# Two-head score steps on two row groups, half-plane maxima, shared mix banks and one pool of eight banks in a four-layer transformer kernel

## The reference, cut to what matters

```python
# block 0 and 1: self attention, cross attention, MLP   (layers 0,1,7 and 2,3,8 of the kernel)
# block 2: cross attention                              (layer 4)
# block 3: windowed self attention, top-k cross attention, SwiGLU   (layers 5, 6, 9)
attn = softmax(einsum('bhnd,bhsd->bhns', q, k) * scale)       # 256 x 256 per head
o = einsum('bhns,bhsd->bhnd', attn, v)
# layer 5: four windows of 64 rows, shifted by 32
# layer 6: top_s, top_i = lax.top_k(scores, 16); softmax over those 16; weighted sum of their v
```

## Time and profile before

| what | value |
|---|---|
| time, three runs | 828.72, 837.08, 854.2 us (median 837.08) |
| span of the profiled execution | 830.0 us, mean granted TensorE clock 0.751 |
| PE / DVE / ACT / POOL busy | 694.1 / 519.2 / 405.8 / 240.4 us |

### The profile page before, as it was taken

The page is one execution under the profiler, slowest core; times in us unless marked ns, Lnnn a source line. Parts: engine busy times, 40 slices in busy tenths (PEclk is TensorE's granted clock), DMA queues, the critical chain, the costliest instruction groups (busy, mean ns, idle before and its releaser), DMA issues.

```text
span 830.0 us, 14443 instructions
## 1 busy us (share of the span) xinstructions
PE 694.1 (84%) x5066; PEld 470.7 (57%) x5066; DVE 519.2 (63%) x1455; ACT 405.8 (49%) x677; POOL 240.4 (29%) x471
## 2 busy tenths in 40 slices
PE   4899997899899898989899887997688968866755
PEld 3675554566566565666566655665555645544533
DVE  3366466635456564646551567778876889899931
ACT  3234555476827476755656570574044713533321
POOL 7511113232333124242112330235010721521302
PEclk9557577798969698969786985597556975886866
DMA  9620203111312401040402060006000220020000
GB/s 346 191 51 3 52 6 65 35 32 23 69 37 52 103 2 43 15 101 8 97 2 53 2 153 1 3 2 145 8 3 1 53 57 3 1 59 0 2 7 6
DMA packets 21700, 39.22 MB, mean 47 GB/s; under 512 B 2496, under 2 KB 6656, under 8 KB 21248
## 3 DMA queue, kind: packets, MB, share of 16 engines
q1 hardware_dynamic: 20912, 37.82, 18.5%
q10 hardware_dynamic: 720, 0.49, 0.2%
HBM read 7.96 MB, written 0.52 MB: 10 GB/s over the span
## 4 chain that ended last, share of the span: by engine, by line
PE 56%; DVE 21%; POOL 7%; DMA 5%; issue 5%; ACT 4%; SPq 2%; POOLq 0%; ACTq 0%; DVEq 0%
PE score L979 14%; PE misc L1025 13%; PE wide L1002 8%; DVE maxima L860 4%; PE wide L1061 4%; DVE left L874 3%; DVE left L882 3%; DVE top L879 3%; PE wide L1036 3%; DVE top L871 3%; DMA qk_stack<-centred 2%; DMA qk_stack<-qk_parts 2%; PE misc L1072 2%; ACT softmax_T L757 2%; SPq L584 2%
## 5 line engine op out<-in xcount | busy, mean ns | idle before, releaser
L860 DVE TENSOR_REDUCE maxima<-score 128x2 f32<-128x512 f32 x320 | 211.8, 687 | 149.0 <-PE score L979 148.0
L757 ACT ACTIVATE softmax_T<-wide 128x1024 f32<-128x1024 f32 (+1 forms) x224 | 211.2, 968 | 106.3 <-PE wide L1002 54.1
L979 PE MATMUL score<-qk_stack 32*128 32x256 f32 (+1 forms) x896 | 215.4, 387 | 53.1 <-DVE maxima L860 20.9
L979 PEld LDWEIGHTS score<-qk_stack 32*128 32x128 f32 x896 | 145.4, 241 | 125.2 <-DVE maxima L860 45.4
L1025 PE MATMUL misc<-softmax_T,values 128*32 128x256 f32 (+1 forms) x1792 | 145.4, 450 | 9.8 <-issue 5.8
L1002 PE MATMUL wide<-qk_stack 32*128 32x256 f32 (+1 forms) x896 | 130.6, 389 | 17.4 <-DMA qk_stack<-centred 9.1
L1002 PEld LDWEIGHTS wide<-qk_stack 32*128 32x128 f32 x896 | 88.3, 240 | 63.4 <-issue 36.3
L686 POOL TENSOR_SCALAR unpicked<-left 128x512 bf16<-128x512 f32 x64 | 39.5, 617 | 191.0 <-DVE left L882 155.1
L1025 PEld LDWEIGHTS misc<-softmax_T,values 128*32 128x32 f32 x1792 | 62.0, 128 | 50.4 <-issue 28.7
L768 ACT ACTIVATE mixed_T<-misc 128x256 f32<-128x256 f32 x112 | 43.6, 389 | 62.0 <-PE misc L1025 61.6
L764 ACT ACTIVATE centred<-misc 16x256 f32<-16x256 f32 (+1 forms) x40 | 14.8, 370 | 104.0 <-PE misc L990 77.8
(11 more groups left out here) (95 smaller groups left out, 802.7 us busy)
## 6 DMA issues: line engine op xcount, KB each, us to landing
qk_stack<-qk_parts SPq DMA_DIRECT2D x112, 256.0 KB, 4.7
weights<-in_w SPq DMA_DIRECT2D x1, 2368.0 KB, 18.3
weights<-in_w SPq DMA_DIRECT2D x1, 1408.0 KB, 13.1
row_biases<-in_rows SPq DMA_DIRECT2D x1, 1088.0 KB, 10.3
weights<-in_w SPq DMA_DIRECT2D x1, 832.0 KB, 8.7
x<-in_x SPq DMA_DIRECT2D x1, 512.0 KB, 4.7
context<-in_ctx SPq DMA_DIRECT2D x1, 512.0 KB, 7.1
out<-x SPq DMA_DIRECT2D x4, 128.0 KB, 2.1
```

The source lines that it names most:

```text
L757: nc.scalar.activation(pT[:, slot, u % 2, :, 0:cols], wide[:, SLOT["wide", step], :, 0:cols], ACT.Exp).then_inc(fin, 1)
L860: nc.vector.tensor_reduce(rows[:, u // 4, u % 4, :], ps.rearrange("p (t k) -> p t k", t=NT), AX_X, ALU.max).then_inc(fin, 1)
L979: ins = nc.tensor.matmul(ps[:, at:at + (P if window else N)], QKS[b][32 * g:32 * g + 32, s, 0, P * t:P * t + P], QKS[b][32 * g:32 * g + 32 ...
```

## The change

- **Score steps of two heads.** `scores` and `topk` steps now take two heads on two neighbouring row groups, 1024 columns in two banks; the four matmuls are written tile by tile with the row groups alternating. 16 steps of a full layer become 8, 8 of the window layer 4, 16 of the top-k layer 8. DVE reduces 1024 columns in one instruction; in top-k each of the four kinds of instruction comes four times in a row. The window layer's `weights` steps go from 8 to 4, of two planes each. The `weights` matmuls alternate row groups too.
- **Maxima in halves.** In full and window layers the maxima of planes 0, 1 and of planes 2, 3 go back separately: two times two transposes, a copy of 8 rows and a DMA, each half with its own semaphore. They are staged in `mixed_T` rather than in `centred`.
- **Two planes share a mix bank.** `values` holds each head in 18 columns (nine and nine zeros), so that two planes add into one bank with 18 used rows per row group. ACT copies twice per layer rather than four times, `divide` takes four transposes rather than eight, and its DVE product is two instructions rather than one.
- **One pool of eight banks.** `wide`, `score` and `misc` become `banks`; a step takes any free bank or pair. The plan lets one scores or topk step be unread at a time (`SCORES_HOLD`) and two mix banks (`MIX_HOLD`). `softmax_T` has three slots, the mask ring two steps of two heads, `context_centred` two slots.
- **The plan.** New costs, a PE cost that depends on a modelled clock, and tables `FIRST` and `EARLY` that shift priorities by kind, batch and layer. The statistics of the context are taken once rather than for each of layers 1 and 4.

```diff
-SLOTS = {"misc": 2, "wide": 2, "score": 2, "qk": 2, "pt": 2, "left": 2, "nm": 8}
+SLOTS = {"qk": 2, "pt": 3, "left": 2, "nm": 2, "zc": 2}
+BANKS.update({k: 2 for k in ("scores", "topk", "weights", "up", "up_gate")})
+SCORES_HOLD, MIX_HOLD = 1, 2
...
+EARLY = [[-23, 13, -73, 16, 45, -31, -10, 13, 0, 113],
...
-LEAD = (120.0, 80.0, 40.0, 0.0)
+LEAD = (141.0, 94.0, 31.0, 23.0)
...
                 elif kind == "scores":
...
-                        nc.vector.tensor_reduce(rows[:, u // 4, u % 4, :], ps.rearrange("p (t k) -> p t k", t=NT), AX_X,
+                        nc.vector.tensor_reduce(mx[:, b, :, first:first + 3:2].rearrange("p t g -> p g t"),
+                                                pair_of(step).rearrange("p g (t k) -> p g t k", t=NT), AX_X,
                                                 ALU.max).then_inc(fin, 1)
...
                 elif kind in ("scores", "topk"):
-                    ps = score[:, SLOT["score", step], :]
-                    g = u % 4
+                    ps = pair_of(step)
+                    planes, groups = heads_of(l, u)
...
                         for t in range(NT):
+                            for g in groups:
...
+                                    to, keys = ps[:, g % 2, N * t:N * t + N], slice(0, N)
+                                ins = nc.tensor.matmul(to, QKS[b][32 * g:32 * g + 32, s, 0, P * t:P * t + P],
+                                                       QKS[b][32 * g:32 * g + 32, s, 1, keys], start=True, stop=True)
...
-                            ins = nc.tensor.transpose(misc[0:NH, P * t:P * t + P], mx[:, b, NH * t:NH * t + NH],
+                            ins = nc.tensor.transpose(bank[0:8, P * t:P * t + P], mx[:, b, t, 8 * u:8 * u + 8],
                                                       ident[:])
...
                 elif kind == "mix":
...
+                            ins = nc.tensor.matmul(bank[32 * g:32 * g + 32, to], V[:, b, t, first:first + 32], weights,
+                                                   start=(t == 0 and u % 2 == 0), stop=(t == NT - 1 and u % 2 == 1),
                                                    tile_position=(0, 32 * g))
...
                     for t in range(NT):
-                        for s in range(4):
-                            n = (4 * t + s) * P
+                        for s in range(2):
+                            n = (2 * t + s) * P
...
-                        sp.dma_start(QKS[b][31::32, :, 0, :].bitcast(F32),
-                                     z[0:NH, b, :, :].rearrange("p t f -> p (t f)")).then_inc(max_in[b], 16)
+                        sp.dma_start(QKS[b][31::32, 2 * u:2 * u + 2, 0, :].bitcast(F32),
+                                     mixT[0:8, b, 2 + u, :]).then_inc(max_in[b][u], 16)
```

More of the change, by code:

```diff
@@ L341, in start_of @@
                 return None
+            if ring == "pt" and len(slots[ring]) == 1:
+                _, b, l, n = t[1]
+                plane = heads_of(l, n)[0][0]
+                if plane % 2 == 0 or ("bank", ("mix", b, l, plane - 1)) not in slot:
+                    return None
             s = max(s, slots[ring][0][0])
@@ L364, in plan @@
         if best is None:
-            raise RuntimeError("the rings are held in a circle")
+            raise RuntimeError("the slots are held in a circle")
         _, s, t = best
@@ L379, in plan @@
         lists[eng].append(step)
+        if eng == "pe":
+            _, got = banks_for(step, s)
+            slot["bank", step] = got[0]
+            had["bank", step] = sorted({reader_of(bank_had[i]) for i in got if bank_had[i]}) \
+                if not (kind == "mix" and u % 2) else []
+            for i in got:
+                bank_at[i], bank_had[i] = None, step
+        else:
+            for i in range(8):
+                if bank_had[i] is not None and bank_at[i] is None and reader_of(bank_had[i]) == t:
+                    bank_at[i] = (s + d / 2 if kind == "topk" else end) + HOP
         ring = takes(t)
@@ L756, in _ @@
-                    cols = P if ATTN[l]["kind"] == "window" else N
-                    nc.scalar.activation(pT[:, slot, u % 2, :, 0:cols], wide[:, SLOT["wide", step], :, 0:cols],
-                                         ACT.Exp).then_inc(fin, 1)
+                    if step == first and HAD["pt", first] is not None:
+                        _, hb, hl, hn = HAD["pt", first]
+                        after(act, "pe", ("mix", hb, hl, heads_of(hl, hn)[0][-1]))
+                    nc.scalar.activation(pT[:, SLOT["pt", first], u % 2, :, :].rearrange("p h n -> p (h n)"),
+                                         pair_of(step).rearrange("p g n -> p (g n)"), ACT.Exp).then_inc(fin, 1)
```

556 lines of the change are left out of this document (317 added, 239 removed), and 3 rows, old and new, of the table EARLY.

## The result

The changed kernel takes 695.59 us in the median (689.61 to 705.07), the kernel before, run beside it, 833.47 (828.72 to 854.2): a ratio of 0.830 with a 95% interval of 0.822 to 0.838. Runs of one kernel differ by up to some 4%, the longer ones at a lower granted clock (689.61 us at 0.811, 705.07 at 0.791), so ratios are taken from the runs at the higher clock, and where medians mix both, spans of profiled executions are given beside them. The profiled execution has a span of 689.1 us and a mean granted clock of 0.814 (before 830.0 and 0.751).

What follows compares the result with a forecast made beforehand. PE's own list was taken to bound the kernel up to the first top-k step, DVE from there to the last. Start 60, then 369 and 296, and end 36 sum to 761 us; range 700 to 815.

Steps and rivals of the forecast that it cites:

- two-head term: Before the first top-k step: score steps of two heads cut rounds on PE from 551 to 430, 34 us off.
- The divide: Before the first top-k step: four of the eight transposes remain, 10 us off PE.
- the halves: Before the first top-k step: maxima in halves add a pair of transposes in each of 18 layers, 9 us on PE.
- 551 rounds: Old order up to the first top-k step: longest row-group queues of score and weights matmuls, priced at 155 us.
- the rival of the falling clock: From 60 us to first top-k step: granted clock falls to about 0.60 or lower; far case 867 us; chance 0.07.
- The price of a round: Before the first top-k step: one matmul on the longest row-group queue costs PE 0.281 us, at mixed clock levels.
- The named waits: PE before the first top-k step: 17.6 us for score banks, 5.3 for the maxima's DMA, 2.2 for a wide buffer.
- the waits that go altogether: Priorities close all PE waits before the first top-k step and DVE waits from there to the last: 707 us; chance 0.17.
- 25 of the 41 us of idle go: PE before the first top-k step: pooled banks, third exponential slot and earlier first half remove 25 us of waits.
- 9 us in B: First to last top-k step: DVE's waits for score matmuls come once for two heads, 9 us off.
- Strict order: Weights steps before the first top-k step took three rounds, now two: 41 us more off, 720 us; chance 0.04.
- The runs do overlap: Rival denied this before the first top-k step: each step pays its own rounds, 43 us more, 804 us; chance 0.10.

Runs made afterwards that it cites:

- the one-head run: Changed kernel with priority tables zeroed and patience 0, score steps of one head again in layers without top-k: 739.77 us.
- the fixed split: Changed kernel with priority tables zeroed and patience 0, score and top-k steps on two fixed pairs of banks, all else on the other four: 833.53 us, ratio 1.008.
- the run in group order: Changed kernel, order of steps untouched, the four matmuls of a score or weights step written row group by row group: 708.1 us.
- the late halves: Changed kernel, tables kept, both halves of the maxima sent back only after a layer's last score step: 733.94 us, ratio 0.885.
- plain priorities: Changed kernel with FIRST and EARLY at zero, the old LEAD head starts and patience 0: 724.64 us, ratio 0.881.

## Why the prediction was wrong

The direction was right, and so were most of the prices of single parts as PE's work; the size was wrong, 761 against 695.59, and the range ended at 700. By the forecast's own stages, counted from the profiled spans:

**Up to the first top-k step: 489 to 386, 103 us, where 60 were forecast.** By the table, PE's work fell from 339 to 297 at a clock of 1.0. At the old clock that would have been 297 / 0.78 = 381 us, 53 less than 434. The clock's rise to 0.87 takes 381 to 341, 40 more. PE's idle time gives 10.

- *Work: 35 forecast (34 + 10 - 9), 53 found.* The two-head term was right as work, 36 by the one-head run, but not as time: that run's stage is not longer for it. The divide was near (8.7 us off, with 10 forecast) and the halves cost less (9 forecast; their transposes take 14.7 in 60 to 386, at the higher clock, where they took 8.2). Two slips did little harm: 551 rounds were counted from the start, but the 166 us begin at 60 and 15.5 more lie before; and a clock that is a mean over time was used as a mean over rounds, which by the same two prices gives 0.264 us a round rather than 0.281, and 32 us rather than 34. (In the rival of the falling clock the same slip makes 459 of what would be 488.) The remaining 15 us or so are spread over other kinds of matmuls, and a mean clock for a stage is too rough to assign them.
- *Clock: 0 forecast, 40 found.* The price of a round was taken at the old mix of clocks, 0.58 full and 0.42 half, and only a fall was weighed as a rival. It went the other way. What raised it is shown only in part: the clock follows both the work that PE is given and the order of the same work (above). That less 32-row work is a reason is not shown: its share of PE's busy time fell (166 of 388 us, now 111 of 294), but with score matmuls doubled the clock is 0.90 against 0.87, and with one-head steps, which need more of them, 0.88 against 0.82.
- *Waits: 25 forecast, 10 found.* The named waits went, 17.6 to 3.6 and 5.3 to 2.2, but others came in their place (exponentials, the reduce ahead of a half's transposes).

**From first to last top-k step: 304 to 265, 39 us, where 8 were forecast.** DVE's work fell by 12 us instead of rising by 1, about half of it in MAX8 (below), the rest mostly instructions that now lie outside this stage. Its idle time fell from 47 to 20. This is the case of the waits that go altogether, which had 0.17 and said that B would lose up to 38; a stage B far below 290 was also named as a sign of being wrong. In A it is not what happened.

**The step that failed** is the pair of lines that put the pool, the third slot and the plan down as PE waits removed, "25 of the 41 us of idle go", and 9 us in B, with the clock held where it was, and gave the plan's tables and its modelled clock no term of their own. By the runs the gain hangs on how the banks are given out: with two pairs set aside for scores the same steps take 833.53 us, no better than before, with one pair 782.55, with the pool 724.64, with the pool and its tables 695.59; the third slot, under the plan's rule for it, is worth 38. Without tables and clocked plan the profiled execution has 737.7 us, 23 below the forecast; the clocked plan brings it to 723.1 and the tables to 689.1, so 49 of the 72 us that the forecast missed are the plan's order. Of the 109 us between the fixed split and the pool, 42 are PE's busy time for the same work (409 and 367, at 0.75 and 0.82), 23 its waits in that stage, and 44 stage B. A table of PE's waits shows only the second of these. The first hides in busy time, as clock. The third shows as DVE's waits, but not for scores: DVE stands 62 us in B instead of 15, mostly for the ends of layers and for masks.

**The rivals.** Strict order falls by the run in group order. The runs do overlap. The clock did not fall. The waits that go altogether came nearest in time (707), by stage B and, unforeseen, the clock; in A the waits that it named did not close, so its nearness there is luck.

**What stays open.** The pieces do not add up exactly: every new plan moves the order, and an edit of small cost may change a run by some 20 us, as the late halves suggest, so the worth of a single part (10 to 20 us for the two-head steps, the clocked plan or the early half) is no more certain than that. How much of the clock's 40 us comes from the order, from shorter waits or from the kind of matmuls was not separated. The pool was not tried in the kernel before, nor the shared mix banks by themselves.

## What to carry to other kernels

A wider step needs the buffers to go with it: price the step together with the ring that it writes to, since here the change without its tables is worth nothing with scores on two fixed pairs (ratio 1.008) and 12% on a pool (0.881), while the two-head steps themselves are worth 1 to 2% on the pool. Where PE bounds a stage whose granted clock lies between the two levels, work out its list at full speed and treat the clock as a term of its own with a range on both sides; held constant here, it cost the forecast 40 us. A table of priorities belongs to the kernel that it was fitted to: worth some 30 us here, this one cost the old kernel 42, so an edit under it is best compared with plain priorities.

## What was not expected of the hardware

- Matmuls whose results are not needed, 31 us of them at full clock up to the first top-k step, made that stage of the old kernel 4 us longer and no more: the granted clock rose from 0.78 to 0.84.
- Each MAX8 takes what it took, 416 ns (418 before), but 128 of them have a busy time of 45.2 us in rows of four where pairs had 48.2: the records of neighbours overlap. The line before:

```profile
L871 DVE MAX8 top<-score 128x8 f32<-128x256 f32 x128 | 48.2, 418 | 17.6 <-PE score L979 9.4 <-POOL unpicked L686 5.1 <-issue 2.8
```

- Four matmuls on two row groups cost the same whether the groups alternate or not. The Trainium skill, "TensorE: Matmul & The Clock Gate", Part 3 ("What overlaps and what doesn't"), has matmuls start and end in program order; the 0.51 us of four group by group and the run in group order, with 0.50, do not bear that out.
